# First attention: the order of SyncE's transfers, the score parts split over two steps and the stack loaded in two halves

## The reference, cut to what matters

```python
qkv = jnp.einsum('bsd,ed->bse', x, w_qkv)
q, k, v = jnp.split(qkv, 3, axis=-1)            # 16 heads of 8 values
q = _apply_rope(q, cos_emb, sin_emb)
k = _apply_rope(k, cos_emb, sin_emb)
scores = jnp.einsum('bhqd,bhkd->bhqk', q, k) / jnp.sqrt(jnp.asarray(hd, x.dtype))
attn = jax.nn.softmax(scores, axis=-1)
out = jnp.einsum('bhqk,bhkd->bhqd', attn, v)
x = _layernorm(x + out.transpose(0, 2, 1, 3).reshape(B, S, D) @ w_out.T + b_out)
```

## Time and profile before

| | |
|---|---|
| time, median of 3 runs | 1552.67 us (1552.26 to 1553.35) |
| time of the profiled execution | 1553.82 us |
| its span | 1551.6 us, 55296 instructions |
| busy, share of the span | PE 95%, DVE 77%, ACT 68%, POOL 62% |
| first attention | from about 37 us to about 541 us of the span |

### The profile page before, as it was taken

How to read it: one execution, slowest core, us unless ns; L and a number is a source line. 1 busy time by engine, 2 the same in 40 slices (tenths; PEclk the granted TensorE clock), 3 DMA queues, 4 the chain that set the end, 5 groups by cost and what they waited for, 6 DMA issues and landing times. The chain is left out here.

```text
span 1551.6 us, 55296 instructions
## 1 busy us (share of the span) xinstructions
PE 1467.2 (95%) x17642; PEld 1145.0 (74%) x17642; DVE 1187.8 (77%) x3338; ACT 1051.0 (68%) x2581; POOL 966.2 (62%) x1160
## 2 busy tenths in 40 slices
PE   5999999999999799979999999999999999998998
PEld 3444555554554399959888888888888888997997
DVE  4777888888888478887878888788878887864666
ACT  2466777777778788856767777777777777774332
POOL 4555565655654067777778877887788777852222
PEclk8799999999999999979999999999999999999999
DMA  5344544454454100122222222222222222200111
GB/s 144 101 131 119 136 128 134 127 136 132 131 136 117 45 32 30 43 87 76 78 72 78 80 76 76 79 80 77 73 81 80 78 70 82 77 23 28 64 64 51
DMA packets 174124, 133.93 MB, mean 86 GB/s; under 512 B 13787, under 2 KB 145126, under 8 KB 174054
## 3 DMA queue, kind: packets, MB, share of 16 engines
q1 hardware_dynamic: 172944, 132.37, 29.4%
q10 hardware_dynamic: 1110, 0.66, 0.1%
HBM read 64.82 MB, written 55.05 MB: 77 GB/s over the span
## 5 line engine op out<-in xcount | busy, mean ns | idle before, releaser
L934 DVE TENSOR_REDUCE shifts<-bank 128x2 bf16<-128x512 f32 x1024 | 684.4, 688 | 169.7 <-PE bank L1086 166.0
L879 ACT ACTIVATE probs<-bank 128x512 f32<-128x512 f32 x1024 | 573.6, 594 | 139.6 <-PE bank L1072 138.2
L1034 PE MATMUL bank<-values,probs 64*128 64x129 f32 x8192 | 579.6, 277 | 3.8 <-DVE o_even L901 0.7
L1034 PEld LDWEIGHTS bank<-values,probs 64*128 64x128 f32 x8192 | 527.1, 188 | 30.6 <-issue 10.8
L1086 PE MATMUL bank<-stack 48*128 48x256 bf16 x2048 | 367.8, 277 | 38.8 <-DMA stack<-score_parts 20.6
L1072 PE MATMUL bank<-stack 49*128 49x256 bf16 x2048 | 376.4, 274 | 8.5 <-ACT probs L879 3.1
L680 POOL TENSOR_TENSOR values<-mix,v_in 128x1024 f32<-128x1024 f32 x128 | 302.0, 2361 | 0.0
L1072 PEld LDWEIGHTS bank<-stack 49*128 49x128 bf16 x2048 | 166.1, 95 | 140.8 <-ACT probs L879 90.2
L689 POOL TENSOR_TENSOR o_odd<-o_odd,scaled 128x256 f32<-128x256 f32 x224 | 163.3, 729 | 161.4 <-ACT scaled L803 161.1
L1086 PEld LDWEIGHTS bank<-stack 48*128 48x128 bf16 x2048 | 156.4, 96 | 61.8 <-DVE shifts L934 24.4
L803 ACT ACTIVATE scaled<-bank,recips 128x128 f32<-128x128 f32 x448 | 137.6, 357 | 88.7 <-DVE recips L928 88.7
(11 more groups left out here) (165 smaller groups left out, 2179.4 us busy)
## 6 DMA issues: line engine op xcount, KB each, us to landing
stack<-score_parts SPq DMA_DIRECT2D x64, 512.0 KB, 4.0
stack<-score_parts SPq DMA_DIRECT2D x256, 96.0 KB
score_parts<-parts SPq DMA_DIRECT2D x256, 64.0 KB, 2.1
score_parts<-parts SPq DMA_DIRECT2D x128, 96.0 KB, 2.3
score_parts<-parts SPq DMA_DIRECT2D x64, 192.0 KB, 2.3
x_in_f<-x_all SPq DMA_DIRECT2D x64, 128.0 KB, 2.0
score_parts<-parts SPq DMA_DIRECT2D x64, 128.0 KB, 2.3
x_in<-in_L_attn_x SPq DMA_DIRECT2D x32, 128.0 KB, 4.3
```

The lines of the kernel that those rows point to most:

```text
L879: act.activation(probs[:, s % RING, :, :].rearrange("p t n -> p (t n)"), s2[s % 2][:, :], ACT.Exp, scale=scale).then_inc(exp_done, 1)
L934: dve.tensor_reduce(shifts[:, :, hf, col], s1_bank(s)[:, :].rearrange("p (t n) -> p t n", t=TILES), op=ALU.max, axis=AX.X, negate=True).th ...
L1034: return pe.matmul(pv_bank(h)[:, q * (D + 1):(q + 1) * (D + 1)], probs[rows, h % RING, t, q * P:(q + 1) * P], values[b.odd][rows, t, h, :] ...
```

## The change

SP's step of the first attention gets an order of its own (`step0`); the second attention keeps the old one (`step1`). `parts_out_in_stack_order` takes a range of the ten transfers. In step i SP now issues: `x_in` of batch i+4; the upper half of the stack of batch i+1; transfers 5 and 6 of the parts of batch i+2; the upper shift row of batch i; transfers 7 to 9; wait for `parts_written`; the lower half of the stack of batch i+2; the lower shift row of batch i+1; wait for `parts_ready` of batch i+3 and for the stack of batch i+1; transfers 0 to 4 of the parts of batch i+3. The number, the size and the content of the transfers stay as they are; no other engine's program is touched.

```diff
+EARLY, MIDDLE = 5, 7
...
-        def parts_out_in_stack_order(b):
+        def parts_out_in_stack_order(b, lo, hi):
-            for parity in range(2):
+            for k in range(lo, hi):
+                parity, k = divmod(k, 5)
...
+        def step0(i, on):
+            leading_in = isinstance(i.half, int) and i.number() < -2
+            starting = isinstance(i.half, int) and i.number() == -2
+            after_start = isinstance(i.half, int) and i.number() == -1
             if on(4):
+                x_block_in(i.plus(4))
+            if on(1) and not after_start:
+                stack_in(i.plus(1), i.plus(-1), lambda k: on(k - 1), 1)
+            if on(2):
+                if starting:
+                    scratch_free(i.plus(2))
+                parts_out_in_stack_order(i.plus(2), 0 if starting else EARLY, MIDDLE)
             if on(0):
                 shift_rows_in(i, 1)
             if on(2):
+                parts_out_in_stack_order(i.plus(2), MIDDLE, writes)
+                wait_apart(sp, parts_written, times(i, 2, n) * (16 * writes))
+                stack_in(i.plus(2), i, on, 0)
+                if starting:
+                    stack_in(i.plus(2), i, on, 1)
+            if on(1):
+                shift_rows_in(i.plus(1), 0)
+            if on(3) and not leading_in:
+                scratch_free(i.plus(3))
+                parts_out_in_stack_order(i.plus(3), 0, EARLY)
...
-        return step
+        return step0 if first else step1
```

More of the change, by code:

```diff
@@ L600, in parts_out @@
                              parts[b.odd][:, Q_PART[s]:Q_PART[s] + m, 0, :]).then_inc(parts_written, 16)
-        def parts_out_in_stack_order(b):
-            for parity in range(2):
+        def parts_out_in_stack_order(b, lo, hi):
+            for k in range(lo, hi):
+                parity, k = divmod(k, 5)
                 split = parts[b.odd][parity * TILE_ROWS:(parity + 1) * TILE_ROWS, :, :, :]
-                for s, m in RUNS[:2]:
+                if k == 4:
+                    k_and_q = split.rearrange("p k e n -> p (k e) n")[:, 1:5:3, :]
+                    sp.dma_start(scratch[b.odd, :, parity, USED - 1, :, :].rearrange("e r n -> r e n"), k_and_q).then_inc(parts_written, 16)
+                    continue
+                s, m = RUNS[k // 2]
+                to = scratch[b.odd, :, parity, s:s + m, :, :].rearrange("e s r n -> e r s n")
+                if k % 2 == 0:
+                    sp.dma_start(to[0], split[:, 0:m, 1, :]).then_inc(parts_written, 16)
+                else:
                     q = K_PART[s]
-                    to = scratch[b.odd, :, parity, s:s + m, :, :].rearrange("e s r n -> e r s n")
-                    sp.dma_start(to[0], split[:, 0:m, 1, :]).then_inc(parts_written, 16)
                     sp.dma_start(to[1], split[:, q:q + 1, 0, :].broadcast_to([TILE_ROWS, m, TOK])).then_inc(parts_written, 16)
-                k_and_q = split.rearrange("p k e n -> p (k e) n")[:, 1:5:3, :]
-                sp.dma_start(scratch[b.odd, :, parity, USED - 1, :, :].rearrange("e r n -> r e n"), k_and_q).then_inc(parts_written, 16)
         def stack_in(b, i, on, hf):
@@ L630, in stack_in, with scratch_free, x_block_in @@
                     sp.dma_start(to.rearrange("q r n -> q (r n)"), src).then_inc(stacked[hf], 16)
-        def step(i, on):
-            if on(4):
[L634 to L642, removed]
+        def scratch_free(b):
+            wait_apart(sp, parts_ready, times(b, 0, n))
+            wait_apart(sp, stacked[0], times(b, -2, n) * (16 * reads))
+            wait_apart(sp, stacked[1], times(b, -2, n) * (16 * reads))
+        def x_block_in(b):
+            if before:
+                wait_for_x(sp, before, TILES, b, "xh_ready")
+            wait_apart(sp, xt_in_psum, times(b, -2, n))
+            if first:
+                wait_apart(sp, added_ready, times(b, -2, n))
+            src = source[b.number(), :, :, :] if first else core.xh_all[:, b.number(), :, :]
+            sp.dma_start(x_in[b.odd][:, :, :], src).then_inc(x_loaded[b.odd], 16)
+        def step0(i, on):
+            leading_in = isinstance(i.half, int) and i.number() < -2
+            starting = isinstance(i.half, int) and i.number() == -2
+            after_start = isinstance(i.half, int) and i.number() == -1
+            if on(4):
+                x_block_in(i.plus(4))
[5 more added lines that the diff above has]
+                parts_out_in_stack_order(i.plus(2), 0 if starting else EARLY, MIDDLE)
             if on(0):
@@ L645, in step, with step1 @@
             if on(2):
[L646 to L654, removed]
+                parts_out_in_stack_order(i.plus(2), MIDDLE, writes)
[8 more added lines that the diff above has]
+                parts_out_in_stack_order(i.plus(3), 0, EARLY)
+        def step1(i, on):
+            if on(4):
+                x_block_in(i.plus(4))
+            if on(0):
+                shift_rows_in(i, 1)
+            if on(2):
+                scratch_free(i.plus(2))
+                parts_out(i.plus(2))
             if on(1):
```

## The result

The changed kernel takes 1536.59 us in the median of 4 runs (1535.67 to 1539.28), the kernel before 1553.01 beside it (4 runs, 1552.26 to 1554.32): a ratio of 0.9893, 95% interval 0.9878 to 0.9909. The prediction was 1537.2 us. The profiled execution took 1539.28 us, the slowest of the four; 1553.82 - 1539.28 = 14.5 us less than that of before.

A forecast was written before the change was run, and what follows sets the result against it. The kernel was taken as bound by a ring through the transfers, closed by the stack's lower half landing ahead of PE's slot 0. Gains of 6.1 + 2.8 + 0.15 + 1.4 + 5.1 = 15.5 us gave 1537.2 us, 8-in-10 range 1533 to 1543.5.

The forecast's parts named there:

- Part 1: Lower half of the stack leaves the ring: issued about 8.0 us after slot 14's addition, not 12.7; slot 0's stall goes.
- what is late next: Slot 1 still waits for DVE's maximum of slot 15; only about 0.3 of 0.95 us gained, loop step floor 14.84.
- rival b: Loop steps fall to the unrolled length, 14.62 us, since slot 0 never waits: 5.3 us more, 1531.9; chance 0.05.
- The sum: Gains of loop 6.1, step 2 2.8, step 28 0.15, step 29 1.4 and step 30 5.1: together 15.5 us.
- rival (a): The tail keeps its stall: the 6.5 us of steps 29 and 30 are not had, 1543.7 us; chance 0.08.
- The median: Median of the runs put 1.15 us below the profiled execution: 1552.67 - 15.5 = 1537.2 us.
- Part 2: Upper half moved to the next step: issued at about 1.2, landed at 5.2, wanted by slot 8 at 8.6; cost nothing.
- Part 3: Shift rows: upper leaves at 3.3, lands 5.6 to 7.6, at worst 8.9, wanted 8.6; cost 0, at worst 0.3 a step.
- Rival (c): Upper shift row, queued behind a half stack and two parts, stalls slot 8 if landing exceeds 5.3 us; 1566 at 6.3; chance 0.05.
- The clock: Granted clock, 0.51 behind the 3.27 us stall, expected full in steps 2, 5 and 30; 1.4 us each in 2 and 30.
- Part 4: Five parts sent a step early: SP waits for POOL, start-up `x_in` goes 3 to 5 us later; counted 0.

The follow-up runs named there:

- experiment 1: Changed kernel, lower half held until the second score of slot 13 is done, with the lower shift row ahead of it: 1548.92 us, ratio to before 0.9968.
- experiment 5: Kernel before, slot 15's first score moved to PSUM bank 2, so slot 1 needs the maximum of slot 13, not 15: 1550.92 us, ratio 0.9996.
- experiment 6: Changed kernel with slot 15's first score moved to PSUM bank 2, so slot 1 no longer needs slot 15's maximum: 1515.7 us, ratio to before 0.9757.
- experiment 2: Changed kernel with no parts sent a step early, parts 0 to 6 going at the step's start behind the upper half: 1538.45 us, ratio 0.9906.
- experiment 3: Changed kernel with the upper half sent behind the lower shift row of the same step instead of in the next step: 1538.64 us, ratio 0.9911.
- 7: Changed kernel with slot 15's first score in PSUM bank 2 and no parts sent a step early: 1514.7 us, ratio 0.9755.
- experiment 4: Changed kernel with all ten parts sent a step sooner, instead of five: 1563.43 us, ratio 1.0071.
- experiment 8: Kernel before, unedited, profiled once more: 1550.43 us, one time.

## Why the prediction was right

**Part 1 and what is late next** hold in the loop: the stall of slot 0 goes, slot 1 takes over behind DVE, the lower half goes at 7.9 and 8.35 in turn (forecast 8.0), a loop step takes 14.85 (forecast 14.84). The undisturbed step of the trace before was the right floor, and the shorter unrolled one (rival b) was not reached. Experiment 1 ties the loop's length to that one issue; experiments 5 and 6 show that the wait which the profile puts down to DVE at 312.25 was the stack's.

**The sum** was 15.5 for 14.4 measured in steps 2 to 30. The term that was mis-sized is step 30: 5.1 for 4.27. Its lower half went at 8.38, near the 8.1 of the text, but slot 0 started only at 493.72, 5.5 us behind the issue. That puts slot 1, 0.24 us behind slot 0, 0.94 later than DVE's release by the text's own offset (493.96 against 492.00 + 1.02), and the step came out at 12.96 instead of 12.1. This is rival (a) in small; its cover was named, and the one thing against it, that only the worst landing passes the limit, was what happened. It came again in experiment 6 (5.7 us) and not in 2, 3 and 7, where this load landed in 3.7 to 3.9. In those three step 29 was longer by the wait for the upper shift row, so steps 29 and 30 together took much the same in all five, 24.8 to 25.4 us. Want of bandwidth it was not: from 491.5 to 492.8 us the changed kernel's DMA engines were busy 0.04 of the time, and still the load landed only at 493.7. Why stays open.

**The median** fits better than the profile of one execution should let one claim. 2.84 us came from step 2, which in the second profile of the kernel before was not long, while step 30 there was 1.8 us longer still. From that profile steps 2 to 30 give 437.08 - 424.56 = 12.5 us. Outside them the start of step 2 came 0.96 us sooner in the changed kernel; it lies anywhere from 78.35 to 84.77 in the kernels above, and three profiles of kernels with the old order of SP gave 81.36, 82.16 and 78.35, so it can't be credited to the change. Step 32 took 9.56 us against 9.05, and 9.05 again in experiments 1 and 3. The profiled execution, forecast at 1538.3, took 1539.28, and the median lies 2.7 us below it, not the 1.15 that the text carried over. The forecast of 1537.2 against 1536.59 is right by its mechanism; that it is off by less than 1 us is luck.

**Part 2** cost nothing, as said, but the upper half went at 1.85 and not 1.2, and in steps that fall on the other half of the loop at 2.3; `x_in` went at 1.28 or 1.65 and not 0.7 to 1.1. SP needs that much more between the last early part and `x_in` than the pitch of the parts gave. Its landing was undersized too: the 4.0 of the earlier trace rows is a median over both halves, and the upper one took 4.7 in the median here. So in the loop it landed at 5.7 to 7.9, 6.8 in the median, and not at 5.2; it was still in time for 8.6. Experiment 4 shows the end of this cover, between 4.1 and 5.55, and the end of that of `x_in`.

**Part 3** was right in the cost (0) and too careful in the price: the landing of the upper shift row was taken as 3.3 us and up to 5.6. Step 29 of the changed kernel, where slot 8 comes early, bounds it in the very order of the text, upper half, two parts, row. Timelines of SP and PE:

```profile
482.28 0.59 SPq L628 DMA_DIRECT2D stack<-score_parts  x1
...
484.19 0.57 SPq L590 DMA_DIRECT2D stack<-shift_rows  x1
...
486.84 0.28 PE L1107 MATMUL bank<-stack 49*128 49x256 bf16 x1
```

The second score of slot 8 does not wait, so the row landed in 486.84 - 484.19 = 2.65 us or less; without a half stack ahead it takes 1.8 (experiments 2 and 3). Rival (c), the slower one, rested on more than 5.3. The text argued from `x_in` behind a half stack, 4.3 us. After the change, with no half stack straight ahead of it, `x_in` lands in 2.2 us. The text also held that the small row can't overtake the half stack. Experiment 4 shows that it can: issued 0.64 us behind the half, the row was there 1.75 us before it. Straight behind a half the row is slow all the same, 2.9 to 4.3 us where PE waited for it in experiment 4.

**The clock** term held: the stretch at 493.5 us shows 1.00, where the kernel before had 0.51, and two more at 82 and 127 us, early in steps 2 and 5, show 1.00 too.

**Part 4** cost nothing, and experiment 2 shows that it gains nothing either, but for some tenths of a us in step 29, where the upper shift row goes in time with it.

## What to carry to other kernels

When the releaser of a wait can't be right by the code, work out the end of every event that it may have waited for; two that end within 0.1 us of each other hide one another, and removing the wrong one gains nothing until the other is gone. In a queue that one engine issues in order, look for the transfer that closes a ring with the bounding engine, and count how many issues stand between its inputs and itself: the gain was in getting seven of the ten in front of the shift row, by whatever means, and in letting the closing transfer go as soon as its inputs were there. A transfer moved to make room has a latest time of its own: in experiment 4 `x_in` and the upper half came 0.5 and 0.8 us after PE was ready for them in the long step shown, and over the run more than the whole gain was gone.

## What the runs showed of the hardware

In these traces the granted clock fell behind the longer stalls of PE and not behind the shorter ones. Behind stalls of 1.05 and 1.31 us (experiment 1, slot 0 of steps 30 and 29) and of 1.60 us (experiment 5, step 6) it stayed 1.00, the 2.4 GHz level. Behind 2.06 us (experiment 8, step 5) it was 0.50, the 1.2 GHz level, from 131 to 133 us; behind 3.27 and 3.58 us (experiment 8, 508 to 511 us) it was 0.51 and 0.50. The stretch behind the 1.31 us:

```profile
491.00:494.00 3.00, 3.00 (x40) 1.69 (x41) 2.75 (x7) 2.75 (x8) 1.20 (x4) 1.00 0.85 229
```

So a stall can cost more than its own length: step 30 of the kernel before took 17.23 us for work that took 12.16 in step 29 after the change, 5.1 more behind a stall of 3.27. And half a us more of stall can cost two: step 6 of experiment 5, behind 1.60 us at the full clock, took 15.74 us; step 5 of the kernel before, behind 2.16 us and with the clock at 0.51 from 133 to 136 us, took 17.90.

The landing of a 128 KB block fell from 4.3 to 2.2 us when no half stack stood straight ahead of it. The lower 512 KB halves landed in 3.7 to 3.9 us in the changed kernel's loop, the upper ones, with two parts issued right behind them, in 3.9 to 5.1; in experiment 3 the upper ones took 3.8 to 4.0. Single lower halves took 5.5 and 5.7. The 4 KB shift row took 1.8 us by itself, 2.65 or less behind a half stack and two parts, and 2.9 to 4.3 straight behind a half stack.
